# A selective state-space layer and a mixture of experts on one core: the state norm summed on TensorE, the state copy moved between two products, the time step's affine map folded away

## The reference, cut to what matters

```python
xc = silu(causal_conv(x_branch))                       # (8, 1024, 512)
dt = soft_clamp(softplus(xc @ W_dt.T + b_dt), 0.001, 0.1, 0.5)
     # soft_clamp(x, lo, hi, s) = tanh((x - c)/r * s)/s * r + c;  here c = 0.0505, r = 0.0495
dt_A = soft_clamp(dt[..., None] * A, -8.0, 8.0, 0.5)   # A: (512, 16)
dA = exp(dt_A);  dB = dt[..., None] * Bp[:, :, None, :]
def step(h, inp):                                      # h: (8, 512, 16)
    h = h * dA_t + dB_t * x_t[:, :, None]
    nrm = sqrt(sum(h * h over channels and states))    # one number for each sequence
    fac = minimum(20.0 / (nrm + 1e-8), 1.0)
    h = where(t % 10 == 0, h * fac, h)                 # every tenth step
    y = einsum('bdn,bn->bd', h, C_t) + D_param * x_t
```

## Time and profile before

| | |
|---|---|
| runs | 2960.3, 2981.33 and 2979.67 us; median 2979.67 |
| the profiled execution | 2959.9 us, its span 2958.1 us |
| busy, share of the span | PE 90%, DVE 84%, ACT 77%, POOL 73% |
| the scan stage | from about 71 us to 2410 us |
| the router and the experts behind it | from about 2460 us to the end |

### The profile page before, as it was taken

One profiled execution on the slowest core, in us unless ns is written; L12 is line 12 of the kernel. 1 busy time (PEld: TensorE's weight loads), 2 busy tenths in 40 slices (PEclk: granted clock), 3 DMA queues, 4 the chain that ended last, 5 costly groups with the idle time before them and its releaser, 6 DMA issues. The chain is left out here.

```text
span 2958.1 us, 50935 instructions
## 1 busy us (share of the span) xinstructions
PE 2648.4 (90%) x16400; PEld 2381.6 (81%) x16400; DVE 2488.2 (84%) x3452; ACT 2265.4 (77%) x5161; POOL 2165.0 (73%) x2239
## 2 busy tenths in 40 slices
PE   4899999999999999999999999999999874899992
PEld 4888888888888898888888988888888774667762
DVE  1999999999999999999999999999999996112123
ACT  6999899899898898988989999989899831111113
POOL 1788888888888888888888888888888872334215
PEclk8999999999999999999999999999999986999996
DMA  2222222222222222222222222222222222134226
GB/s 64 64 71 74 76 67 79 73 70 79 69 77 77 67 79 70 73 76 71 77 74 66 79 73 74 77 71 76 75 65 81 66 61 88 42 90 100 56 45 238
DMA packets 153969, 225.67 MB, mean 76 GB/s; under 512 B 46056, under 2 KB 92776, under 8 KB 152552
## 3 DMA queue, kind: packets, MB, share of 16 engines
q1 hardware_dynamic: 131208, 188.98, 22.1%
q0 software_dynamic: 9216, 12.59, 2.4%
q10 hardware_dynamic: 13280, 20.86, 2.1%
HBM read 189.26 MB, written 33.05 MB: 75 GB/s over the span
## 5 line engine op out<-in xcount | busy, mean ns | idle before, releaser
L642 POOL TENSOR_TENSOR H<-H,CB 128x640 f32<-128x640 f32 x832 | 1262.9, 1526 | 273.9 <-DVE H L479 268.3
L479 DVE TENSOR_TENSOR_SCAN H<-DA,PM 128x704 f32<-128x704 f32 x832 | 1320.8, 1608 | 20.8 <-ACT DA L276 1.2
L394 ACT ACTIVATE DA<-DT,SM 128x160 f32<-128x160 f32 x3328 | 1115.9, 425 | 1.6 <-POOL DT L610 0.3
L664 PE MATMUL YB<-H,ID 128*128 128x160 f32 x6656 | 1049.2, 310 | 0.5 <-POOL H L642 0.5
L664 PEld LDWEIGHTS YB<-H,ID 128*128 128x128 f32 x6656 | 987.8, 191 | 16.7 <-issue 11.2
L454 DVE TENSOR_TENSOR PM<-PM,BB 128x640 f32<-128x640 f32 x832 | 642.3, 817 | 5.1 <-issue 0.4
L276 ACT ACTIVATE DA<-DA 128x2560 f32<-128x2560 f32 x208 | 485.3, 2334 | 1.6
L1119 POOL DMA_INDIRECT YA<-YS,IG x48 | 75.2, 1566 | 239.7 <-ACT YS L942 228.1
L628 POOL TENSOR_TENSOR FC<-SN,HALF 128x4 f32<-128x4 f32 x206 | 212.4, 1031 | 47.8 <-DVE SN L485 35.3
L670 PE MATMUL PA<-XN,WIN 128*128 128x160 f32 x832 | 153.8, 332 | 58.5 <-POOL XN L622 57.0
L763 PE MATMUL PZ<-WO,Z 128*80 128x256 f32 x832 | 188.2, 379 | 0.1
(11 more groups left out here) (164 smaller groups left out, 3654.0 us busy)
## 6 DMA issues: line engine op xcount, KB each, us to landing
BB<-Bd SPq DMA_DIRECT2D x208, 320.0 KB, 3.5
CB<-Cd SPq DMA_DIRECT2D x208, 320.0 KB, 3.4
W<-in_w ACTq DMA_DIRECT2D x16, 1024.0 KB, 7.5
XT<-in_xT SPq DMA_DIRECT2D x52, 160.0 KB, 2.2
XR<-in_xp SPq DMA_DIRECT2D x416, 20.0 KB
X2d<-VV SPq DMA_DIRECT2D x416, 20.0 KB
YA<-VV SPq DMA_DIRECT2D x416, 20.0 KB
HI<-YA SPq DMA_DIRECT2D x6, 1024.0 KB, 9.9
```

Source lines behind the costliest of these rows:

```text
L394: eng.activation(DA[:, c0:c0 + 2, :, a, m, 1:11].rearrange("p c b t -> p b c t"), DT[:, j % 2, a].rearrange("p b (c t) -> p b c t", c=2), ...
L479: eng.tensor_tensor_scan(H[:, q % 3, u], a0, DBX(u), 0.0, ALU.mult, ALU.add).then_inc(s_scan, 1)
L642: eng.tensor_tensor(h, h, cb, ALU.mult).then_inc(s_hc, 1)
L664: mm = eng.matmul(yv, ID[:], hv[:, :, :, n, 0:10], start=False, stop=n == 15)
```

## The change

It has five parts.

1. The norm. L705 was one product of `MEAN` (all entries 1/256) with the 256 squares of a unit (4 sequences x 64 blocks and states), and VectorE reduced 256 numbers to 4. Now four products with 64 columns each, one for a channel block, accumulate in the same 64 columns, and VectorE reduces 64 numbers to 4.
2. The copy of the carried state stands between the two B products and no longer behind both.
3. The affine map of the time step (L610, GpSimd) is gone. ScalarE writes the tanh straight into `DT`; the factor and the offset are folded into the scale and a bias (`AO`) of the 64 tanh, into the copy of B (`scale=S1`), and into dt*x, which becomes a `scalar_tensor_tensor` with the same two inputs.
4. GpSimd's `XN` product is emitted in slot 14 behind the carried state, no longer in slot 15.
5. TensorE projects the gate's second half (PZ) in slot 14, behind the first six `y_sum` products, and no longer in slot 13.

```diff
@@ scalar_program
-                        eng.activation(BS[:], pv[0:16], ACT.Copy).then_inc(s_bcs, 1)
+                        eng.activation(BS[:], pv[0:16], ACT.Copy, scale=S1).then_inc(s_bcs, 1)
...
-                            eng.activation(TA[:], TA[:], ACT.Tanh, bias=CST[:, 2:3], scale=KD).then_inc(s_dth, 1)
+                            if j >= 2:
+                                eng.wait_ge(s_u, 2 * j - 1)
+                            eng.activation(DT[:, j % 2], TA[:], ACT.Tanh, bias=CST[:, 2:3], scale=KD).then_inc(s_dt, 1)
...
-                                scale=AS[:, a, m:m + 1]).then_inc(s_z64, 1)
+                                bias=AO[:, a, m:m + 1], scale=AS[:, a, m:m + 1]).then_inc(s_z64, 1)
@@ vector_program
-                eng.tensor_tensor(U(c), DT[:, j % 2, :, :, t], XC[:, j % 2, :, :, t], ALU.mult).then_inc(s_u, 1)
+                eng.scalar_tensor_tensor(U(c), DT[:, j % 2, :, :, t], S0 / S1, XC[:, j % 2, :, :, t],
+                                         ALU.add, ALU.mult).then_inc(s_u, 1)
...
                         mult(q, u)
+                        carry(q, u)
                         mult(q, u + 1)
-                        carry(q, u)
@@ gpsimd_program
-                    if s == 14 and ok(i + 2):
-                        j = i + 2
-                        eng.wait_ge(s_dth, j + 1)
-                        if j >= 2:
-                            eng.wait_ge(s_z64, 64 * (j - 1))
-                            eng.wait_ge(s_u, 2 * j - 1)
-                        eng.tensor_scalar(DT[:, j % 2], TA[:], 0.0495 / 0.5, 0.0505, ALU.mult, ALU.add).then_inc(s_dt, 1)
...
-                    if s == 15 and ok(i + 3):
...
+                    if s == 14 and ok(i + 3):
                         j = i + 3
                         eng.wait_ge(s_rs, j + 1)
                         if j >= 2:
                             eng.wait_ge(s_gt, 2 * (j - 1))
                         eng.tensor_tensor(XN[:, j % 2], XT[:, j % 2], RST[:].unsqueeze(1).to_broadcast([128, 2, 160]),
+                                          ALU.mult).then_inc(s_xn, 1)
@@ tensor_program
-                        eng.matmul(NP(p), MEAN[:], SQ[:], start=True, stop=True).then_inc(s_nrm, 1)
+                        for a in range(4):
+                            mm = eng.matmul(NP(p), MEAN[:], SQ[:, :, 16 * a:16 * a + 16], start=a == 0, stop=a == 3)
+                        mm.then_inc(s_nrm, 1)
                     if u == 2:
                         y_sum(q - 1, 0, 6)
                     if u == 3:
                         y_sum(q - 1, 6, 11)
+                    if s == 14 and ok(i + 1):
+                        j = i + 1
+                        wait_free(eng, users_pz, i, GT0)
+                        project(j, 512, PZ).then_inc(s_gt, 1)
...
-                    if s == 13 and ok(i + 1):
-                        j = i + 1
-                        wait_free(eng, users_pz, i, GT0)
-                        project(j, 512, PZ).then_inc(s_gt, 1)
```

More of the change, by code:

```diff
@@ L52, in ssm_phase @@
         NW = SM[:, 92:94]
+        AO = sb("AO", [128, 4, 16])
         SC = SM[:, 94:96]
@@ L95, in ssm_phase @@
             sem("sq"), sem("ms"), sem("root"), sem("rs"), sem("xb"), sem("th"), sem("ex"))
-        s_bcs, s_ln, s_dth, s_tg, s_z64, s_da, s_x2t, s_hsq = (
-            sem("bcs"), sem("sp"), sem("dth"), sem("tg"), sem("z64"), sem("da"), sem("x2t"), sem("hsq"))
+        s_bcs, s_ln, s_dt, s_tg, s_z64, s_da, s_x2t, s_hsq = (
+            sem("bcs"), sem("sp"), sem("dt"), sem("tg"), sem("z64"), sem("da"), sem("x2t"), sem("hsq"))
         s_halo, s_sgh, s_dx, s_dxh, s_hc = sem("halo"), sem("sgh"), sem("dx"), sem("dxh"), sem("hc")
-        s_min, s_dt, s_xn, s_pow, s_fac, s_car = (
-            sem("min"), sem("dt"), sem("xn"), sem("pow"), sem("fac"), sem("car"))
+        s_min, s_xn, s_pow, s_fac, s_car = sem("min"), sem("xn"), sem("pow"), sem("fac"), sem("car")
         s_ve, s_sd, s_x2 = sem("ve"), sem("sd"), sem("x2")
@@ L111, in ssm_phase @@
         KD = 0.5 / (0.0495 + 1e-8)
-        PRE_C, PRE_CV, PRE_W, N_PRE = 9, 27, 29, 34
+        S0, S1 = 0.0505, 0.0495 / 0.5
+        PRE_C, PRE_CV, PRE_W, N_PRE = 9, 27, 29, 35
         loads = [
@@ L132, in NP @@
         def NP(q):
-            return YB[1 - q % 2][:, 256:512]
+            return YB[1 - q % 2][:, 256:320]
         def two(j):
@@ L326, in scalar_program @@
                         j = i + 2
-                        if j > 0:
-                            eng.wait_ge(s_dt, j)
                         for n, (p, m) in enumerate(((PA, 1), (PZ, 0))):
@@ L426, in vector_program @@
             eng.wait_ge(s_prea, 2)
-            eng.tensor_scalar(AS, AS, -0.5 / (8.0 + 1e-8), None, ALU.mult).then_inc(s_pre, 1)
+            eng.tensor_scalar(AO[:], AS, -0.5 / (8.0 + 1e-8), S0, ALU.mult, ALU.mult).then_inc(s_pre, 1)
+            eng.tensor_scalar(AS, AS, -0.5 / (8.0 + 1e-8), S1, ALU.mult, ALU.mult).then_inc(s_pre, 1)
             eng.wait_ge(s_prea, 3)
@@ L616, in gpsimd_program @@
                         eng.tensor_copy(SG[:, j % 2, :, :, 0:1], SG[:, 1 - j % 2, :, :, 20:21]).then_inc(s_sgh, 1)
-                    if s == 15 and ok(i + 3):
-                        j = i + 3
-                        eng.wait_ge(s_rs, j + 1)
-                        if j >= 2:
-                            eng.wait_ge(s_gt, 2 * (j - 1))
-                        eng.tensor_tensor(XN[:, j % 2], XT[:, j % 2], RST[:].unsqueeze(1).to_broadcast([128, 2, 160]),
-                                          ALU.mult).then_inc(s_xn, 1)
                     if u == 2 and 1 <= q <= NQ - 2:
@@ L635, in gpsimd_program @@
                                           ALU.mult).then_inc(s_car, 1)
+                    if s == 14 and ok(i + 3):
+                        j = i + 3
+                        eng.wait_ge(s_rs, j + 1)
+                        if j >= 2:
+                            eng.wait_ge(s_gt, 2 * (j - 1))
+                        eng.tensor_tensor(XN[:, j % 2], XT[:, j % 2], RST[:].unsqueeze(1).to_broadcast([128, 2, 160]),
+                                          ALU.mult).then_inc(s_xn, 1)
                     if live:
```

## The result

The changed kernel takes 3293.02 us, the median of 4 runs (3290.17 to 3294.27), against 2977.64 for the kernel before beside it (4 runs). The ratio is 1.1069, with a 95% interval of 1.1031 to 1.1107. The direction was forecast, the size was not: +315 us where the prediction had +127 on its profiled execution, and above its range of 3025 to 3140. So the experiments are compared by their ratio to the kernel before of their own session. Where a ratio and the length of a pass say different things, by up to one point, the text says so: the profile of the kernel before is from an execution of 2959.9 us. The profiled execution of the changed kernel has a span of 3292.3 us (2958.1 before), so that 334 us have to be found between the two traces.

The account below looks back on a forecast made before the run. VectorE (98.6% busy) was taken as the bound, TensorE 5% behind. Loop +71 and clock +56 made +127 us: 3087 on the profiled 2959.9, 3107 on the median, middle 3097 us; range 3025 to 3140.

Parts of the forecast that it names:

- the price of the tanh's bias operand: ScalarE's 64 tanh a pass: a bias from SBUF taken as free, at most 0.03 us each, 1.9 us a pass.
- inside ScalarE's 8% of idle time: ScalarE: at 0.03 us each the 64 tanh's 1.9 us a pass would fit its idle time.
- The wait moves to `SQ`: TensorE before slot 0's norm: one wait of about 2.4 us for ScalarE's squares, none for `XN` or VectorE.
- The loop closes whatever VectorE saves: TensorE and ScalarE, PZ through norm to next PZ: 46.75 us a pass, 1.39 more, +71 us over 51 passes.
- The clock: TensorE after the new wait: half clock in three passes of four, 1.5 us each, 1.1 us a pass, +56 us.
- the bound of "all": TensorE's clock loss, upper bound: every pass loses 1.7 us (half of 3.4), +87 us.
- ScalarE waits 1.7 us for PZ: ScalarE in slot 14: a wait of about 1.7 us for the gate's second half, where it was 0.37.
- VectorE and its copy: VectorE: copy between B products saves 0.19 us, shorter reduction 0.2, in four units 1.56 us a pass, to 43.8 us.
- dt\*x in another form costs nothing: VectorE's dt*x as `scalar_tensor_tensor`: no cost, bounds -0.6 and +0.5 us a time.
- Rival 2: TensorE's narrow norm goes by its columns, the loop does not bind: 2935 to 2955 us, or 2880 to 2900; chance 0.10.
- (b): Rival theory after the result, tanh and TensorE: the bias costs little and the clock carries the loss; no chance given.
- Rival (c): Rival theory after the result: the TensorE and ScalarE loop is much dearer than worked out; no chance given.

Follow-up runs that it names:

- gate late + narrow norm, clock held, filled kernel: Parts 1, 2, 4 and 5 in the kernel before, without part 3, plus ten idle TensorE products ahead of slot 0's norm: 2994.21 us, ratio 1.0111.
- + bias, clock held: The changed kernel plus idle TensorE products, twelve ahead of slot 0's norm and eight in slot 9's wait: 3167.82 us, ratio 1.06.
- no-fold kernel: Parts 1, 2, 4 and 5 in the kernel before, without part 3 (the time step's affine map stays): 3082.97 us, ratio 1.0412.
- first filled kernel: The changed kernel plus twelve idle TensorE products of 128 columns ahead of slot 0's norm only: 3244.55 us, ratio 1.0895.

## Why the prediction was right in direction and wrong in size

**The step that failed is the price of the tanh's bias operand**, put at nothing with bounds of 0 and 0.03 us, "since both come in by the same way". It is 0.0925 us, as measured. On 64 tanh this is 5.9 us a pass, where ScalarE had 45.36 - 41.5 = 3.9 us idle, and not all of that in one place. The argument "inside ScalarE's 8% of idle time" was made for the 1.9 us of the upper bound, which no run tests, and fails for three times as much. At held clock a pass grows by 49.29 - 46.00 = 3.3 us. ScalarE's idle time falls from 46.00 x (1 - 1706.12 / 1900) = 4.7 us to 2.1, so that 2.6 of the 5.9 us are hidden and 3.3 are paid. By the ratios this is 1.06 - 1.0111, 4.9 points; by the passes it is 168 us or 5.7 points, and the two sessions differ by 29 us in the kernel before.

The trace of before had the price in two rows of equal shape that I did not set side by side (the same view by line, 400 to 2300):

```profile
L366 ACT ACTIVATE RST<-RST,CST 128x160 f32<-128x160 f32 x42 | 17.3, 412 | 0.0
L374 ACT ACTIVATE RST<-RST 128x160 f32<-128x160 f32 x42 | 13.4, 320 | 0.0
```

L366 takes its bias from SBUF, L374 takes none, both have 128x160 elements in and out: 92 ns. One is a logarithm and the other an exponential, but the function hardly counts: L362 and L370, a logarithm and a tanh of 128x640 elements, both take 829 ns. "No row shows that price" was therefore wrong. The bound that I used, a tenth of the nearest row, came from no row at all.
The Trainium skill has the same number in "ScalarE: Activation LUTs", section "What ACT_TABLE_LOAD costs": each per-partition pointer operand adds about 93 ns. The runs agree with it, with 91 to 94 here. As an estimate by that page, 64 x 0.093 x 51 = 304 us would have been the loss had nothing been hidden.

The account of a pass in microseconds, averaged over the whole loop, each step the difference of two kernels:

```
before                                     45.36
gate late + narrow norm, clock held        46.00   +0.64
  + bias, clock held                       49.29   +3.29
  + clock, as it is in the changed kernel  51.77   +2.48
```

Point by point:
- *The wait moves to `SQ`*: right. 2.50 us in the no-fold kernel (predicted 2.4), no wait for `XN` or VectorE. In the changed kernel it is 3.05, longer by the 0.56 us that six tanh grow.
- *The loop closes whatever VectorE saves*: right in kind, too large. It gives +0.64 us a pass with the clock held, not +1.39. One part is in the norm's records: eight go by in 0.83 or 0.84 us to the next start, not 0.90, and the wide product in 0.43, so +0.41 and not +0.47 a time, 0.24 in four. Another is the stretch from PZ's start to the norm's, 1.39 + 5.38 = 6.77 us in the prediction and 6.60 in the no-fold kernel (1227.08 less 1220.48 in its timeline), 0.17. The rest lies in the averages, which take in shorter passes at the ends of the loop. In the steady stretch a pass without a drop lasts 45.37 us before (1216.02 in the earlier trace rows to 1261.39 in the earlier trace rows) and 46.33 in the filled kernel (1232.04 to 1278.37). So the loop was 46.33 us where 46.75 were worked out, and 0.24 + 0.17 account for 0.41 of the 0.42.
- *The clock*: right in kind, too small. 1.5 us in three passes of four were assumed; the no-fold kernel loses 47.74 - 46.00 = 1.74 us a pass on average, the bound of "all" (1.7). The clock falls in each of its passes; most last 47.99 us in the steady stretch, and five last 49.6, where the half clock is twice as long. The kernel before had the drop in 9 passes between 400 and 2300 us, not in the 12 that the prediction took from a rounded 0.99. Loop and clock erred in opposite directions, so that the sum without the bias, +127, met the measured +122 by luck more than by its terms.
- *ScalarE waits 1.7 us for PZ*: 90.6 / 44 = 2.1 in the no-fold kernel. In the changed kernel only 0.7, since ScalarE comes later.
- *VectorE and its copy*: right where VectorE binds. Product, copy and product take 1.64 us, the reduction 0.21, and a pass of the kernel of parts 2 and 4 is 0.61 us shorter, where 0.76 were worked out; the move of `XN` has a part in these 0.61 that no run separates. The prediction read the section "The DRAIN you can't avoid" of "VectorE: DVE Perf Modes" in the Trainium skill as speaking for no gain. The section also says that a next operation that is not held starts earlier, which agrees with the starts in the earlier trace rows.
- *dt\*x in another form costs nothing*: right, to 0.2 us in 3083, together with the missing `DT` step.
- *Rivals*: each took the bias for free too, so none came near. Rival 2 had VectorE bind at 2880 to 2900; that is where parts 1, 2 and 4 end (2895) when the gate stays.

Of the rivals after the result, (b) holds in part: the clock carries 4.7 of the 10.7 points by the ratios, 4.2 by the passes. But without the bias the clock carries 3.0, so that the rest, 1.2 to 1.7, is the bias's as well. Rival (c) falls: the loop was cheaper than worked out.

## What to carry to other kernels

Before an affine step is folded into an operand of many small instructions, multiply the operand's price by their number, and take the price from two rows of equal shape, one with and one without it: here one 0.72 us instruction of GpSimd, for which the tanh had waited 0.3 us in the whole run, was traded for 64 x 0.0925 us on an engine that had 3.9 us left. An estimate that is small for one instruction deserves a row, not a guess, when 64 of them meet in a pass. And a wait that moves onto TensorE in one piece can be paid twice, in its length and in the clock behind it; where it can't be removed, idle products in it are worth trying (here 3.0 and 4.7 points back), in every such wait of the pass.

## What the runs showed of the hardware that was not expected

- An operand from SBUF costs ScalarE 91 to 94 ns an instruction, the scale like the bias: 331, 425 and 516 to 518 ns for 128x160 elements with none, one and two.
- Records of 64 and 128 columns with a 128 x 128 weight load follow each other alike: 8 in 0.83 us and 4 in 0.45. Between these two sizes the narrower product saves TensorE nothing.
- The half clock followed a wait of 2.50 us in each pass of the no-fold kernel, one of 3.05 in each pass of the changed kernel, and one of 2.02 in each pass of the first filled kernel. In the changed kernel it followed the wait of 2.01 us in 9 of 36 passes only, and then it lasted 6.8 us behind the other wait, not 3.4. In the one trace of the kernel with only the gate moved it followed a wait of 2.50 us in 23 of 40 passes.
- The kernel with only the gate moved has two times, 2961 to 2966 us and once 2998, the latter seen with a lowered clock. What decides between them is open.
